# Perceiver block on one core: row tiles in staggered orders, context chunks turned in row halves, a shift's second copy on VectorE

## The reference

```python
x = x + _L0_xattn_ref(_layernorm(x), ctx_512, ctx_512, ...)   # the block that is changed
x = x + _L0_attn_ref(...)    # linear attention
x = x + _L0_ffn_ref(...)
x = x + _L1_xattn_ref(_layernorm(x), ctx_512, ctx_512, ...)
x = x + _L1_attn_ref(...)
x = x + _L1_ffn_ref(...)     # attention and experts
```

```python
qh = (q @ Wq + bq).reshape(B, LQ, HEADS, D_K).transpose(0, 2, 1, 3)
kh = (k @ Wk + bk).reshape(B, LKV, HEADS, D_K).transpose(0, 2, 1, 3)
vh = (v @ Wv + bv).reshape(B, LKV, HEADS, D_K).transpose(0, 2, 1, 3)
scores = jnp.einsum('bhqd,bhkd->bhqk', qh, kh) * scale
attn = jax.nn.softmax(scores, axis=-1)
out = jnp.einsum('bhqk,bhkd->bhqd', attn, vh)
```

## Time and profile before

| | |
|---|---|
| Time, median of 3 runs | 1392.46 us (1392.43 to 1394.41) |
| Profiled execution, its own time | 1394.46 us |
| Its span, first to last instruction | 1392.7 us |
| TensorE busy | 1325.9 us, 95% |
| VectorE busy | 1057.2 us, 76% |
| ScalarE busy | 951.0 us, 68% |
| GpSimd busy | 286.8 us, 21% |

### The profile page before, as it was taken

One profiled execution on the slowest core, in us unless ns is written; L12 is line 12 of the kernel. 1 busy time (PEld: TensorE's weight loads), 2 busy tenths in 40 slices (PEclk: granted clock), 3 DMA queues, 4 the chain that ended last, 5 costly groups with the idle time before them and its releaser, 6 DMA issues.

```text
span 1392.7 us, 33516 instructions
## 1 busy us (share of the span) xinstructions
PE 1325.9 (95%) x13666; PEld 846.1 (61%) x13666; DVE 1057.2 (76%) x2114; ACT 951.0 (68%) x2027; POOL 286.8 (21%) x321
## 2 busy tenths in 40 slices
PE   7799999999999999999999898889999999989998
PEld 4355555556655555565555555547448999856666
DVE  4777888887888888888888878536877678678757
ACT  5367888888888878888876666654886554448721
POOL 3354223332233223322332000000012100002110
PEclk9899999999999999999999999998989999999999
DMA  5847454365453454543446221021202310356000
GB/s 172 187 140 199 116 128 103 92 142 130 122 141 78 119 136 123 135 106 99 108 96 197 51 52 37 1 62 51 71 24 76 111 57 1 98 134 135 2 1 31
DMA packets 98794, 134.60 MB, mean 97 GB/s; under 512 B 11024, under 2 KB 74128, under 8 KB 92688
## 3 DMA queue, kind: packets, MB, share of 16 engines
q1 hardware_dynamic: 98640, 132.45, 37.8%
HBM read 94.15 MB, written 38.27 MB: 95 GB/s over the span
## 4 chain that ended last, share of the span: by engine, by line
PE 83%; DVE 6%; ACT 6%; DMA 2%; issue 1%; SPq 1%; POOL 1%; ACTq 0%; DVEq 0%
PE psum L605 18%; PE psum L551 17%; PE psum L537 8%; PE psum L2285 4%; PE psum L582 3%; PE psum L586 3%; PE psum L2259 3%; ACT probs L895 2%; PE psum L1379 2%; PE psum L3004 2%; PE psum L1776 1%; PE psum L3014 1%; PE psum L275 1%; PE psum L746 1%; PE psum L660 1%
## 5 line engine op out<-in xcount | busy, mean ns | idle before, releaser
L786 DVE TENSOR_REDUCE peaks<-psum 128x1 f32<-128x512 f32 x1024 | 641.2, 684 | 120.1 <-PE psum L537 118.3
L895 ACT ACTIVATE probs<-psum 128x512 f32<-128x512 f32 x1024 | 539.3, 600 | 170.0 <-PE psum L551 163.6
L551 PE MATMUL psum<-queriesT,keysT 64*128 64x256 bf16 (+1 forms) x4096 | 465.3, 271 | 24.9 <-ACT probs L895 24.9
L551 PEld LDWEIGHTS psum<-queriesT,keysT 64*128 64x128 bf16 (+1 forms) x4096 | 284.4, 95 | 162.1 <-issue 93.6
L537 PE MATMUL psum<-keysT,queriesT 64*128 64x512 bf16 x1024 | 315.9, 383 | 9.4 <-DMA keysT<-key_parts 4.5
L605 PE MATMUL psum<-probs,values 128*17 128x256 f32 x4096 | 273.0, 382 | 0.0
L605 PEld LDWEIGHTS psum<-probs,values 128*17 128x17 f32 x4096 | 100.5, 96 | 111.5 <-ACT probs L895 55.9
L1065 POOL CAST key_parts<-key_f 128x512 bf16<-128x512 f32 x57 | 34.7, 610 | 467.7 <-ACT key_f L940 430.9
L537 PEld LDWEIGHTS psum<-keysT,queriesT 64*128 64x128 bf16 x1024 | 92.9, 93 | 55.9 <-DVE peaks L786 45.9
L2072 ACT ACTIVATE weights<-psum,peaks 128x256 f32<-128x256 f32 x128 | 58.6, 484 | 12.4 <-DVE peaks L1941 12.2
L2285 PEld LDWEIGHTS psum<-ctx_nat,ring 128*128 128x128 f32 x512 | 64.6, 191 | 3.6 <-ACT ring L2420 0.7
(11 more groups left out here) (325 smaller groups left out, 1919.9 us busy)
## 6 DMA issues: line engine op xcount, KB each, us to landing
keysT<-key_parts SPq DMA_DIRECT2D x186, 256.0 KB, 5.7
key_parts<-key_parts SPq DMA_DIRECT2D x90, 256.0 KB
ctx_nat<-in_ctx_dram SPq DMA_DIRECT2D x32, 256.0 KB, 3.1
ctx_in<-in_ctx_dram SPq DMA_DIRECT2D x24, 256.0 KB, 5.5
ctx_turned<-ctxT SPq DMA_DIRECT2D x24, 256.0 KB, 6.5
ctx_T<-ctx_turned SPq DMA_DIRECT2D x12, 512.0 KB, 4.0
qk_parts<-early_weights SPq DMA_DIRECT2D x24, 128.0 KB
q_parts<-q_parts SPq DMA_DIRECT2D x20, 128.0 KB
```

What stands on the lines that cost most here:

```text
L551: made = e.matmul(ps[:, e2 * S:(e2 + 1) * S], self.keysT[own, plane, i % RING, kt * P:(kt + 1) * P], self.queriesT[own, plane, u % 2, g, : ...
L786: e.tensor_reduce(self.peaks[:, i % 2, j * QT + qt, c:c + 1], k.ps(("max", n)), AX.X, ALU.max).then_inc(*self.peaked.up(n))
L895: e.activation(self.probs[:, t % RINGP, 2 * j * S:(2 * j + 2) * S], k.ps(("scores", t, j)), ACT.Exp).then_inc(*self.exped.up((t, j)))
```

## The change

It has three parts.

1. Each row tile gets its own order. The odd slot holds only one maximum (head 1's) and only head 1's first two score matmuls; the last two move to the next even slot, behind half part 0. The even slot then has head 1's four scores, its own two maxima and the next odd slot's maximum of head 0, then head 0's four scores with half part 1 after the first. ScalarE copies a half before the last exponential of the even slot, not after it. VectorE reduces before its jobs in all slots.
2. A context chunk of batches 1 to 3 is turned as eight transposes of 64 rows, four on each row tile, into two banks (`turn_ctx`). ScalarE copies each bank.
3. Of the two copies of a turned shift, one stays on ScalarE and the other goes to VectorE, after its reductions of that slot; there is a semaphore for each.

```diff
+        def odd_slot(t):
+            ahead = self.maxima(t)
+            score(t, 0, 0)
+            for n in ahead[1:]:
+                find_max(n, t)
+            score(t, 0, 1)
+            score(t, 1, 0)
+            score(t, 0, 2)
+            score(t, 1, 1)
+            score(t, 0, 3)
+
+        def turn_ctx(t, b, c):
+            halves = [misc(t, ("ctx", b, c, h), (self.ctx_kept, (b, c) if h else ("half", b, c))) for h in range(2)]
+            w.wait_ge(self.ctx_here[(b * CH + c) % 2], (b, c))
+            for i in range(4):
+                for h, ps in enumerate(halves):
+                    own = slice(h * HALF, (h + 1) * HALF)
+                    made = e.transpose(ps[:, i * HALF:(i + 1) * HALF], self.ctx_in[own, (b * CH + c) % 2, i, :], ident[own, own])
+                    if i == 3:
+                        made.then_inc(*self.ctx_half_made[h].up((b, c)))
+
+        def even_slot(t):
             halves = [job for job in self.due.get(t, ()) if job[0] in HALF_JOBS]
-            w.wait_ge(self.shiftT_kept, t // SLOTS)
+            for kept in self.shiftT_kept:
+                w.wait_ge(kept, t // SLOTS)
             w.wait_ge(self.ones_in, 0)
+            for half in halves:
+                half_job(t, 0, *half)
+            if t:
+                score(t - 1, 1, 2, 3)
+            score(t, 1, 0, 1, 2)
+            ahead = self.maxima(t)
+            for n in ahead[:1]:
+                find_max(n, t)
+            score(t, 1, 3)
+            for n in ahead[1:]:
+                find_max(n, t)
+            for n in self.maxima(t + 1)[:1]:
+                find_max(n, t)
+            score(t, 0, 0)
+            for half in halves:
+                half_job(t, 1, *half)
+            score(t, 0, 1, 2, 3)
...
         # VectorE
-            if 0 <= t < TOTAL and t % 2:
-                jobs(t)
-                for n in reversed(self.maxima(t)):
-                    peak(n)
-            else:
-                for n in self.maxima(t):
-                    peak(n)
-                jobs(t)
+            for n in self.maxima(t):
+                peak(n)
+            jobs(t)
+                elif job == "turn shift":
+                    own = slice(HALF + LOW, HALF + TALL)
+                    w.wait_ge(self.shiftT_made, i)
+                    e.tensor_copy(self.queriesT[own, REST, u % 2, g, :], k.ps(("shiftT", i)).bitcast(BF16)[own, 0:S]).then_inc(
+                        *self.shiftT_kept[1].up(i))
...
         # ScalarE
                 for j in order(t):
+                    if t % 2 == 0 and j == 0:
+                        jobs(t, HALF_JOBS)
                     w.wait_ge(self.scored[j], (t, j))
...
+                        for h in range(2):
+                            w.wait_ge(self.ctx_half_made[h], (b, c))
+                            e.activation(turned[:, :, h, :], k.ps(("ctx", b, c, h))[:, 0:S].rearrange("p (i n) -> p i n", n=HALF),
+                                         ACT.Copy).then_inc(*self.ctx_kept.up((b, c) if h else ("half", b, c)))
```

More of the change, by code:

```diff
@@ L317 @@
 HALF_JOBS = "fill half", "make half"
+OTHER_JOBS = ("turn ctx", "fill keys", "split rest", "turn x", "keep queries", "make queries", "split queries", "turn shift",
+              "make values", "stream")
+ALL_JOBS = HALF_JOBS + OTHER_JOBS
 def order(t):
@@ L554, in score @@
                 made.then_inc(*self.scored[j].up((t, j)))
[L556 to L561, removed]
         def half_job(t, part, job, *a):
@@ L623, in even_slot @@
-            half_job(t, 0, *half)
-            score(t, early, 0, 1, 2, 3)
-            for n in maxima:
-                find_max(n, t)
[L627 to L645, removed]
+            for half in halves:
+                half_job(t, 0, *half)
@@ L715, in tensor @@
         for t in range(FIRST, TOTAL + 3):
-            maxima = self.maxima(t)
+            if t == TOTAL:
+                score(t - 1, 1, 2, 3)
             if t < 0 or t >= TOTAL:
-                for n in maxima:
+                for n in self.maxima(t):
                     find_max(n, t)
@@ L725, in tensor @@
                 jobs(t)
-                odd_slot(t, maxima)
+                odd_slot(t)
             else:
-                even_slot(t, maxima)
+                even_slot(t)
                 jobs(t)
@@ L905, in keep_sums, with jobs @@
                 e.activation(self.outT[:, :], k.bank(SUMS)[:, 0:S], ACT.Copy).then_inc(*self.outT_kept.up(i))
-        def jobs(t):
+        def jobs(t, only):
             for job, *a in self.due.get(t, ()):
+                if job not in only:
+                    continue
                 if job == "turn ctx":
@@ L913, in jobs @@
                         continue
[L914 removed]
+                    if b == 0:
+                        w.wait_ge(self.ctx_made, (b, c))
                     if b >= 2:
@@ L1101, in sync @@
                     if n >= CH + 2:
-                        w.wait_ge(self.ctx_made, divmod(n - 2, CH))
+                        before = divmod(n - 2, CH)
+                        for made in self.ctx_half_made if before[0] else (self.ctx_made,):
+                            w.wait_ge(made, before)
                     e.dma_start(self.ctx_in[:, n % 2, :, :],
```

35 lines of the change are left out of this document (19 added, 16 removed).

## The result

The changed kernel took **1421.0 us** (median of four, 1419.7 to 1425.6). The kernel before, run beside it, took 1392.5 (1391.3 to 1394.4). The ratio is 1.0209, with a 95% interval of 1.0183 to 1.0236: slower by 2.1%. The forecast was 1424, in a range of 1406 to 1438.

What follows compares the result with a forecast made beforehand. Bound: TensorE's two tile queues and their waits for late VectorE and ScalarE results. Terms 15 + 8.5 + 11 - 2 + 1 - 1 gave about +32: 1426 for the profiled execution, 1424 against the median; range 1406 to 1438.

Steps and rivals of the forecast that it cites:

- plain pairs: Odd slot plus following even slot without rare jobs: 1.93 for 1.95 to the value product, about 97 times, -2 us.
- chunk: Context chunk turned in halves waits for ScalarE's copy of the same slot's half until 2.56: +0.63 each, 23 times, +15.
- heads: Gather of a finished group's heads: VectorE scales after the reduction, so the next maximum starts at 1.61; +0.35, 24 times, +8.5.
- shift, without and with chunk: Shift transposes wait for the key half's copy: +0.55 (12 groups without chunks), +0.36 (12 with), together +11.
- after slot 396: Pairs without halves: 45 at -0.14, against seven gathers, six shift ends and lin steps scaled after the reductions; +1 together.
- first eight pairs: The first 8 pairs gain 0.14 each, like pairs without halves: -1.
- only the chunks cost: Low end of the range: late chunk pairs let VectorE and ScalarE catch up; +12, 1404.
- the upper bound of the transposes: Each small chunk transpose takes 0.22 instead of 0.13: 0.36 more per chunk, +8 on top of the sum.
- the wait at 1.10: Tile 0 stands from 1.10 to 1.17 until the odd slot's maximum, whose bank its second maximum takes, is reduced.
- The rival of program order: Program order holds where one tile's run is long: each pair about 0.35 longer, 1490; chance 0.03.
- The rival of free banks: Banks come free in time, the half's copy seen before 1.93, so chunk and shift don't wait: 1370; chance 0.11.
- Overlapping waits: Rival: a late chunk pair lets VectorE and ScalarE catch up, only chunks cost: +12, 1404; chance 0.10.

Runs made afterwards that it cites:

- the kernel with all three repairs: Changed kernel with VectorE's jobs between the odd slot's two reductions, and shift and context chunks each turned one slot later: 1383.8 us, ratio 0.9919.
- the best version: Kernel before with second shift copy on VectorE, staggered order from slot 409, chunks in halves one slot later, ScalarE's half copy before the last exponential: 1378.9 us.
- the one before it: Kernel before with second shift copy on VectorE and, only from slot 409, the staggered order with VectorE's jobs between the reductions: 1381.6 us, ratio 0.9907.

## Why the prediction was right, and where it was off

The direction came from the part of the argument that asked which user of the four banks comes four before, and when that one's reader is done. All three places stood where the forecast put them. Against the measured account:

| term | forecast | measured |
|---|---|---|
| plain pairs | -0.02 each: -2 | -0.01 each (2.938 to 2.927): -0.9 |
| chunk | +0.63 x 23 = +15 | +0.42 x 22 (3.525 to 3.944), +0.38 once: +9.6 |
| heads | +0.35 x 24 = +8.5 | +0.34 x 20, +0.28 once, -0.39 x 3: +5.8 |
| shift, without and with chunk | +0.55, +0.36: +11 | +0.47, +0.35: +9.7 |
| after slot 396 | +1 | +3.5 |
| first eight pairs | -1 | +0.7 |

The measured terms add up to the +28.4. Three terms were forecast 9 too high in all and three 5 too low, so a part of the closeness of 1424 to 1421 is errors that offset each other. The ends of the range aren't quite the sums that it names, which are 1404 (only the chunks cost) and 1432 (the upper bound of the transposes), not 1406 and 1438.

- **The chunk** is the term that was mis-sized most. The wait was forecast to 0.01. What I lacked was the price of a 64 x 64 transpose on one tile, which I had put beside the full-size 0.13; the four on each tile start at 403.25, 403.36, 403.43 and 403.49 in the trace, so 0.11 and then 0.06 to 0.07 apart, and both tiles take theirs at once. From the last one's start to the value product are 0.16: together 0.40, for the 0.61 of the forecast. That is the 0.21 by which the product was earlier (2.96 for 3.17).
- **The heads** came close to the forecast at 21 of 24. At the other three, where a batch ends and VectorE has a bias to add, the old order was itself longer (4.30) and the new one is not (3.91; the pair behind it takes 3.12 for 2.94). I had not looked at these apart.
- **The shift** came as forecast with a chunk, 0.08 smaller without. The four transposes were too dear in the forecast: the value product starts at 420.14, 0.01 behind the first of them, where I had 0.11; the next pair, at 3.00, pays 0.07 of it back.
- **After slot 396** a plain pair gains 0.21, more than 0.14: without halves only four users go round four banks, so a maximum finds its own bank of the pair before, and the wait at 1.10 that I had left in isn't there. The steps of the second block cost more than the 1.5 that I gave them; the experiment that moves VectorE's jobs ahead of a reduction gets 7.8 back there.
- **The first eight pairs** lost 0.7; I had counted them as pairs without other work, which they aren't: the one with the first group's shift takes 5.18 for 4.56.
- **The rival of program order** did not occur. In the plain pair above L580's second pass starts at 412.14, behind a score of the other tile at 412.03 that stands later in the program, and tile 0's maximum at 412.36, right behind the half, with five scores of tile 1 ahead of it in the list, the last of which starts 0.01 behind it. The Trainium skill ("TensorE: Matmul & The Clock Gate", Part 3, The mechanism) has matmuls strictly first in, first out; between two row tiles these rows disagree, at the new spacing too.
- **The rival of free banks** did not occur; the kernel with all three repairs comes near that state by other slots (1383.8, not 1370). **Overlapping waits** did not occur: the pair behind a chunk is not shorter than it was.
- The parts don't add. Alone they are worth 1.0234, 1.0159 and 0.9941, all three 1.0209. Beside part one, halves bring 0.19 a chunk instead of costing, since there the whole chunk waits for the same copy already (the rows are 17.6 and 11.6 with either). Part three brings nothing beside it: pairs 16 to 192 take 581.9 with part one alone and 581.8 with parts one and three. The likely reason is that the new wait at the shift covers what the old copy cost; no run takes the two apart.

What stays open is how much of the best version's gain over the one before it (5.3 in pairs 16 to 192) comes from each of its three edits, which were only run together.

## What to carry to other kernels

Where several jobs share buffers strictly in turn, a job that takes one buffer more, or stands one place further on, gets a new predecessor: list for each job the user that many places before it and the time at which that one's reader ends, before changing the order. A rare job costs its whole wait, since both tiles stand behind one list, while an order made for the common slot gave 0.01 us a pair here; it gave 0.21 only in the pairs without halves, where four users go round the four banks. Try the rare jobs in the neighbouring slot first: three small moves of rare jobs, in one kernel, took the ratio from 1.021 to 0.992 here.

## What the runs showed of the hardware

- Transposes of 64 x 64 float32 on two row tiles at once: eight in 0.46 us with the length of the last, 0.06 to 0.11 apart on a tile; four of 128 x 128 on the full array took 0.66.
- What follows the block is the same work each time and takes a time that goes with the granted clock: from the last value product to the end 465.3 us before and 465.4 in the changed kernel, both at 0.97, and 459.5 at 0.99 in the one with the heads' scaling moved. In the attention, like pairs agree to about 0.01 us where the clock is full, and a stretch at 0.50 added 4.0 us (10.2 long, in the run with the chunks one slot later) and 3.5 (6.8 long, in the one with the new order from slot 409) where it fell. So the account above goes by pairs and not by totals, and a long pair is first looked up in the granted clock.
